# Top-32 attention and convolution stage: statistics, norms, reciprocals and the reversal put on other engines and into other steps

## The chip, the cores and the metric

One core of one Trainium2 chip runs the whole program. The metric is the device time of one execution in microseconds (us). The engines are TensorE (PE), VectorE (DVE), ScalarE (ACT), GpSimd (POOL) and SyncE (SP, which issues the DMAs here). They run their own instruction streams and meet in semaphores.

## The reference, cut to what matters

The program is four layers of gated cross-attention and feed-forward on x of 32 x 128 x 128 with a context of 32 x 128 x 96. The change touches the attention of layer 1 (32 batches of 128 tokens, 4 heads of 32):

```
scores = einsum('bthd,bghd->bhtg', Q, K) / sqrt(DH)
topv, topi = top_k(scores, 32);  probs = softmax(topv)
attn = zeros_like(scores).at[bi, hi, ti, topi].set(probs)
c_t = einsum('btg,bgd->btd', attn.mean(axis=1), V) * text_mask
x = layernorm(x_text, g_norm_in, b_norm_in)
scale_in, shift_in = split(c_t @ W_film_in + b_film_in, 2)
x = x * (1 + mod_gate * scale_in) + mod_gate * shift_in
y = s4d(x, ...)        # a causal convolution over the 128 tokens, one kernel per channel
```

Then a second FiLM with scale_out and shift_out, a residual and a feed-forward layer follow, and the later layers.

## The kernel before, in words

`build` runs six stages one after the other. `stage_film` is `film_in` (attention, first norm, FiLM; output x3, tokens in partitions, [128, channel, batch]) and then `convolve`. Between the two all engines meet in a barrier.

`film_in` works on pairs of batches (16 pairs) and on groups of 4 batches (8 groups, 512 columns). Every engine's order is written out by hand: a loop over p from -5 to 18 in which each engine does a fixed list of parts, for pair p+1, p, p-1 or p-2. The main parts:

- VectorE (lines 1455 to 1496): for pair p, four rounds of 8 MAX8 (`dve.max`, the 8 largest of 128 scores, one per head and batch) and 8 MATCH_REPLACE, which overwrites these 8 in `left`. After four rounds the 32 largest are gone from `left`. Ahead of an odd pair stand `group_stats` and `group_moments` (four BN_STATS and seven small operations by which the halves of BN_STATS are put together) for the norm of a later group, and three small operations for `rstd2`, the second variance (the norm is applied on a norm).
- ScalarE (1402 to 1453): for pair p-1 the exponential of `left` (`exb`), for pair p that of all scores (`exa`), each with the sum over the keys as a second output; for pair p+1 the evacuation of the scores (`sc`); for a group the evacuation of `xnT` (p odd) or of `kT` and `qT` (p even); for pair p-2 those of `wT`, `aT` and the FiLM product `fo`, two of each.
- GpSimd (1268 to 1337): the shift of the softmax (`shift`, from the first maximum); for a group the power for `rstd`, the application of the norm to four batches (`xn`, line 1297), two copies into `k.mean1` and `k.rstd1`, and the second norm with its gain and bias (x2); for pair p-1 the two differences (`share` = tota - totb, and exa - exb, which leaves the 32 largest), the power -1 (line 1322), two products; for pair p-2 the FiLM: x2 times f, plus f, written into `k.x3[:, :, i]`, 128 bytes between neighbours (1336).
- TensorE (1339 to 1400): for pair p-2 the head mean and its transposition (`wT`), for pair p+1 the scores, for a group the transpositions of `xn` and the K and Q products (banks 6 and 7), for pair p-2 `aT` and the FiLM product. All 8 banks of PSUM are in use; the scores have one buffer (banks 0 to 3).
- SP: the contexts, four of the eight chunks of Toeplitz matrices (1 MB each) at the start, and after each batch the half of `fo` that the next stage needs, to DRAM (`fo_dram`). It waits for the last of these at the end.

After the last pair VectorE quantizes a weight for a later stage (1498 to 1525), in exchange with TensorE.

`convolve` (1528 to 1584) first reverses x3 in the tokens, by a product with an exchange matrix `k.flip`: 8 chunks of 512 columns over TensorE, each evacuated by ScalarE into x3 in place. Then, chunk after chunk, 16 Toeplitz products with 32 columns of weights each, an evacuation, 4 transpositions, a copy by VectorE back into x3. Four chunks of Toeplitz matrices are loaded at its start (`v_late`).

Of the kernel before, what the change touches and what calls it, by code (L numbers as in the profile page):

```python
# [5 lines left out]
F32 = mybir.dt.float32  # L6
# [10 lines left out]
G = 4  # L17
# [1163 lines left out]
def stage_film(nc, w, ps, k):  # L1181

    with ExitStack() as ctx:
        k.toep = ctx.enter_context(nc.sbuf_tensor("v_toep", [128, EARLY, CH, 128], F32))
        once = ctx.enter_context(OneTime(nc, "v_in_"))
        k.toep_in = [once(f"toep_in{i}") for i in range(CHUNKS)]
        film_in(nc, w, ps, k)
        convolve(nc, w, ps, k)
# [5 lines left out]
def film_in(nc, w, ps, k):  # L1194
# [8 lines left out]
    TAKES = 2 * H * ROUNDS  # L1203
    with ExitStack() as ctx:
        def tmp(name, shape, dt=F32):
            return ctx.enter_context(nc.sbuf_tensor("c_" + name, shape, dt))

        nm = Norm(lambda n, s: ctx.enter_context(nc.sbuf_tensor(n, s, F32)), "c")
        rstd2 = tmp("rstd2", [128, 2, G])
# [4 lines left out]
        minus, tshare = tmp("minus", [128, H]), tmp("tshare", [128, B])  # L1214
        sc, left = tmp("sc", [128, 4, H, 128]), tmp("left", [128, 4, H, 128])
# [8 lines left out]
        stats, halves, square, mean, ve, rstd, rr, vr, ve2, rstd2_done, kept = (  # L1224
            once(n) for n in ("stats", "halves", "square", "mean", "ve", "rstd", "rr", "vr", "ve2", "rstd2_done",
                              "kept"))
# [9 lines left out]
        fo_out = [once(f"fo_out{i}") for i in range(2)]  # L1236
# [5 lines left out]
        norm = dict(stats=Signal(stats, 0, 2 * G, k.apart), halves=Signal(halves, 0, 6, k.apart),  # L1242
                    square=Signal(square, 0, 4, k.apart), mean=Signal(mean, 0, 2, k.apart),
                    ve=Signal(ve, 0, 2, k.apart))
# [7 lines left out]
        def _(sp):  # L1252
# [4 lines left out]
            for i in range(B):  # L1257
                if i in (10, 18):
                    e = i // 8 + 1
                    sp.wait_ge(aT_ps, 8 * (e - 1))  # L1260
                    sp.dma_start(cx[:, e % 2], c_dram[:, 8 * e:8 * e + 8, :]).then_inc(cx_in[e], 16)
                sp.wait_ge(fo_done, i + 1)
                sp.dma_start(k.fo_dram[:, i:i + 1, :].rearrange("s b c -> s (b c)"),
                             fo[:, i % 2, 256:512]).then_inc(fo_out[i % 2], 16)
            for a in range(2):
                sp.wait_ge(fo_out[a], 16 * B // 2)

        @block.gpsimd
        def _(pool):
# [3 lines left out]
            pool.memset(minus[:], -1.0).then_inc(consts, 1)  # L1273
            pool.tensor_scalar(tshare[:], k.tmask[:], 1.0 / H, None, ALU.mult).then_inc(consts, 1)
            pool.wait_ge(consts, 3)
# [4 lines left out]
            for p in range(FIRST, LAST):  # L1280
                for i in pair(p):

                    pool.wait_ge(top_done, TAKES * p + H * (i % 2 + 1))
                    if i >= 4:
                        pool.wait_ge(exb_done, H * (i - 3))
                    pool.tensor_scalar(shift[:, i % 4, :], first[:, i % 2, :, 0], -SCALE, None,
                                       ALU.mult).then_inc(shift_done, 1)
                if (p + 4) % 2 == 0 and 0 <= (p + 4) // 2 < GROUPS:
                    g = (p + 4) // 2
                    u = g % 2  # L1290
                    pool.wait_ge(ve, g + 1)
                    pool.tensor_tensor(nm.rstd[:, u], nm.ve[:, u], k.half[:, 0:G], ALU.pow).then_inc(rstd, 1)
                    pool.wait_ge(rstd, g + 1)
                    if g >= 4:
                        pool.wait_ge(x3_done, G * (g - 3))
# [3 lines left out]
                    pool.tensor_copy(k.mean1[:, G * g:G * g + G], nm.mean[:, u]).then_inc(kept, 1)  # L1299
                    pool.tensor_copy(k.rstd1[:, G * g:G * g + G], nm.rstd[:, u]).then_inc(kept, 1)  # L1300
# [14 lines left out]
                for i in pair(p - 1):  # L1315
                    a = i % 2
                    pool.wait_ge(exb_done, H * (i + 1))
                    pool.tensor_tensor(share[:, a, :], tota[:, i % 4, :], totb[:, a, :],
                                       ALU.subtract).then_inc(tot_done, 1)
# [1629 lines left out]
```

## Time and profile before

| | us |
|---|---|
| median of 3 runs | 1514.41 (1513.07 to 1514.45) |
| profiled execution | 1510.89 |
| its span, first to last instruction | 1509.1 |
| mean granted TensorE clock | 0.849 of full |
| opening of `film_in` | 207.1 to 223.4 |
| loop of 16 pairs on VectorE | 223.4 to 472.9 |
| rest of `film_in` to `convolve`'s first product | 472.9 to 494.3 |
| `convolve` to the first product of `stage_mix` | 494.3 to 518.7 |

Times are read from the span's start. A duration is that of the instruction; neighbours on an engine can overlap a little, so eight operations of 0.39 us may take 3.18 us together. The granted clock is 0.5 or 1.0 at any moment, which are TensorE's levels of 1.2 and 2.4 GHz; between them stand means over a stretch. The ends of matmuls are modelled.

### The profile page before, as it was taken

To read this page: it belongs to the slowest core of one execution; us is meant where nothing else is said; L and a number is where in the kernel's file an instruction comes from. 1 tells how busy PE (TensorE), PEld (TensorE's weight loads), DVE (VectorE), ACT (ScalarE), POOL (GpSimd) and SP (SyncE) were. 2 spreads that over 40 slices of the span, in tenths; PEclk is the share of its full clock that TensorE was granted. 3 is DMA by queue.
4 is the path that set the end of the run, shared out by engine and by line. 5 is a ranking of instruction groups with operands and counts; after the bars stand their busy time and mean duration, and the time that the engine had idled before them with its cause. 6 is when DMAs were issued, how large, how long until landed. Compare 5 with 4: busy or idle time off the path is not lost. (4 is left out here: it accounts for less than half of the span.)

```text
span 1509.1 us, 30794 instructions
## 1 busy us (share of the span) xinstructions
PE 1195.9 (79%) x10535; PEld 812.8 (54%) x10535; DVE 1009.3 (67%) x3919; ACT 684.5 (45%) x1990; POOL 594.7 (39%) x806
## 2 busy tenths in 40 slices
PE   4767654766676669885698988689999969999997
PEld 3433322443444445554476767356667657776765
DVE  6767759999996279862577777677776544444442
ACT  3343335566665344421244444356666633333332
POOL 4677576888867155530323231233433310000000
PEclk7789865566666779996699999799999979898988
DMA  6301050010000511100000000000000000000001
GB/s 164 90 1 43 1 134 1 15 32 16 25 22 22 161 43 27 30 16 16 1 3 3 3 3 3 1 1 1 2 2 2 1 1 0 1 0 0 0 0 56
DMA packets 63678, 35.54 MB, mean 24 GB/s; under 512 B 23925, under 2 KB 61424, under 8 KB 63538
## 3 DMA queue, kind: packets, MB, share of 16 engines
q1 hardware_dynamic: 62234, 33.45, 8.5%
q8 instruction: 76, 1.25, 0.4%
q14 instruction: 64, 0.52, 0.1%
q10 hardware_dynamic: 1304, 0.33, 0.1%
HBM read 25.21 MB, written 6.42 MB: 21 GB/s over the span
## 5 line engine op out<-in xcount | busy, mean ns | idle before, releaser
L2821 DVE SCALAR_TENSOR_TENSOR k_X<-ps,m_gt,k_X 128x128 f32 (+1 forms) x256 | 72.1, 345 | 123.0 <-PE ps L2720 123.0
L2750 ACT ACTIVATE m_hid<-ps,k_b 128x512 f32<-128x512 f32 x128 | 81.8, 684 | 134.9 <-PE ps L2720 127.7
L2720 PEld LDWEIGHTS ps<-k_w,m_hid 128*128 128x128 f32 x1024 | 123.1, 192 | 26.8 <-issue 17.2
L2711 PE MATMUL ps<-m_xnT,k_w 128*128 128x512 f32 x256 | 127.8, 630 | 1.1 <-DVE m_lg L2766 1.1
L2720 PE MATMUL ps<-k_w,m_hid 128*128 128x128 f32 x1024 | 123.4, 275 | 0.0
L2399 POOL TENSOR_TENSOR l_p<-l_p,l_rsum 128x512 f32<-128x512 f32 x64 | 65.2, 1039 | 139.4 <-DVE l_rsum L2658 139.4
L2259 DVE TENSOR_REDUCE g_top<-ps 128x8 f32<-128x1024 f32 x64 | 75.4, 1220 | 50.6 <-PE ps L2127 50.6
L1494 DVE MATCH_REPLACE8 c_left<-c_top,c_left 128x128 f32<-128x128 f32 x384 | 104.5, 354 | 0.0
L2519 ACT ACTIVATE l_p<-ps,l_shift 128x128 f32<-128x128 f32 x256 | 91.4, 389 | 21.3 <-DVE l_shift L2603 20.2
L2207 ACT ACTIVATE g_pT<-ps 128x1024 f32<-128x1024 f32 x64 | 62.0, 1021 | 84.8 <-PE ps L2143 84.8
L711 PE MATMUL ps<-f_expT,f_xeT 128*128 128x512 f32 x128 | 69.9, 675 | 29.3 <-DVE k_X L1089 29.0
L1488 DVE MAX8 c_top<-c_left 128x8 f32<-128x128 f32 x384 | 81.9, 349 | 0.0
L1367 PE MATMUL ps<-c_kT,c_qT 32*128 32x128 f32 x256 | 22.9, 440 | 72.9 <-ACT c_sc L1427 71.6
L121 POOL TENSOR_TENSOR m_rstd<-m_ve,k_half 128x8 f32<-128x8 f32 x4 | 6.6, 1639 | 186.0 <-DVE m_ve L114 186.0
L2711 PEld LDWEIGHTS ps<-m_xnT,k_w 128*128 128x128 f32 x256 | 47.5, 204 | 41.1 <-issue 39.6
L842 ACT ACTIVATE f_part<-ps,f_wf 128x128 f32<-128x128 f32 x128 | 36.3, 368 | 71.4 <-issue 46.1
L1353 PEld LDWEIGHTS ps<-k_ident,c_exa 128*128 128x128 f32 x256 | 48.9, 283 | 23.0 <-issue 12.4
L1494 DVE MATCH_VALUE_LOAD c_left<-c_top,c_left 128x8 f32 x384 | 60.1, 158 | 0.0
L711 PEld LDWEIGHTS ps<-f_expT,f_xeT 128*128 128x128 f32 x128 | 24.4, 214 | 66.0 <-DVE k_X L1089 46.3
L1367 PEld LDWEIGHTS ps<-c_kT,c_qT 32*128 32x128 f32 x256 | 14.9, 268 | 82.6 <-issue 77.1
L2519 ACT ACTIVATION_READ_ACCUMULATOR l_p<-ps,l_shift 128x1 f32 x256 | 58.8, 230 | 0.0
L1089 DVE SCALAR_TENSOR_TENSOR k_X<-ps,f_wf,k_X 128x128 f32<-128x128 f32 x128 | 44.6, 349 | 19.8 <-PE ps L711 15.8
(535 smaller groups left out, 3284.3 us busy)
## 6 DMA issues: line engine op xcount, KB each, us to landing
v_toep<-kpad SPq DMA_DIRECT2D x4, 1024.0 KB, 10.5
fo_dram<-c_fo SPq DMA_DIRECT2D x32, 128.0 KB, 1.7
v_late<-kpad SPq DMA_DIRECT2D x4, 1024.0 KB, 10.1
d_fo<-fo_dram SPq DMA_DIRECT2D x8, 512.0 KB, 3.6
k_X<-in_x SPq DMA_DIRECT2D x8, 256.0 KB, 3.4
out<-k_X SPq DMA_DIRECT2D x4, 512.0 KB, 5.4
f_cx<-in_ctx SPq DMA_DIRECT2D x4, 384.0 KB, 5.6
c_cx<-in_ctx SPq DMA_DIRECT2D x4, 384.0 KB, 4.7
```

Source lines behind the costliest of these rows:

```text
L711: pe.matmul(ps[:, 4 + (2 * b + h) % 3, :], xeT[:, t % 2, u, cols], expT[:, 4 * h:4 * h + 4, :].rearrange("p e d -> p (e d)"), start=True, ...
L1353: m = pe.matmul(ps[:, 4 + a, 0:128], exa[:, i % 4, h, :], k.ident[:], start=h == 0, stop=h == H - 1)
L1488: dve.max((first if r == 0 else top)[:, a, h, :], (sc if r == 0 else left)[:, i % 4, h, :]).then_inc(top_done, 1)
L1494: dve.match_replace(left[:, i % 4, h, :], (first if r == 0 else top)[:, a, h, :], (sc if r == 0 else left)[:, i % 4, h, :], TAKEN).then_in ...
L2207: act.activation(pT[:, n % 2, 2 * h:2 * h + 2, :].rearrange("p a n -> p (a n)"), ps[:, 4 + 2 * h:6 + 2 * h, :].rearrange("p a n -> p (a n) ...
L2259: dve.tensor_reduce(top[:, (n + 1) % 2, :].rearrange("p (r c) -> p r c", r=R)[:, 2 * h:2 * h + 2, 0:R], ps[:, 2 * h:2 * h + 2, :].rearrang ...
L2399: pool.tensor_tensor(p[:, n % 3, 4 * a:4 * a + 4, :], p[:, n % 3, 4 * a:4 * a + 4, :], rsum[:, n % 3, 4 * a:4 * a + 4].rearrange("p (h o) ...
L2519: act.activation(p[:, i % 3, h, :], ps[:, 2 * (i % 2) + a, 128 * b:128 * b + 128], ACT.Exp, bias=shift[:, i % 2, h:h + 1], scale=SCALE, ac ...
L2711: pe.matmul(ps[:, 4 * u + q, :], k.w1_3[:, e, 128 * q:128 * q + 128], xnT[:, u], start=True, stop=True).then_inc(s["hid_ps"].sem, 1)
L2720: m = pe.matmul(ps[:, 4 * u + 2 + e % 2, j * S:j * S + S], hid[:, u, q, j * S:j * S + S], k.w2_3[:, e, q, :], start=q == 0, stop=q == 1)
L2750: act.activation(hid[:, u, q, :], ps[:, 4 * u + q, :], ACT.Gelu, bias=k.b1_3[:, 2 * e + q:2 * e + q + 1]).then_inc(s["hid"].sem, 1)
L2821: dve.scalar_tensor_tensor(out=xj[u][j], in0=ps[:, 4 * u + 2 + e % 2, j * S:j * S + S], scalar=gt[:, u, j, e:e + 1], in1=xj[u][j], op0=ALU ...
```

## The change

- **Statistics.** VectorE's `group_moments` is replaced by one BN_AGGREGATE per batch (`dve.bn_aggr`), which gives mean and variance into `k.mv1`; the addition of eps, the power and the `rstd2` arithmetic are GpSimd's.
- **Norms.** The application of the norm moves from GpSimd to VectorE for groups 0 and 1, and to ScalarE for the others (an ACTIVATE with scale rstd and bias -mean x rstd, at the end of its even steps).
- **Reciprocals.** GpSimd's two powers -1 per pair become one RECIPROCAL of 128x8 on VectorE, for pair p-1, ahead of round 2 of pair p, behind a wait for GpSimd's differences. GpSimd makes these differences right behind the shift.
- **Opening.** The statistics of groups 0 and 1 and their applications come first on VectorE, those of group 2 stand in round 1 of pair 0; the K product and evacuation of group 0 come before its transpositions.
- **Reversal.** GpSimd writes the FiLM result contiguously into `y` (two batches). Three steps after the pair, at the end of TensorE's step, one product of 256 columns reverses it in bank 7, and ScalarE copies it into x3 with `p (a c) -> p c a`. The eight products and evacuations of `convolve` go.
- **Loads.** `sc` and `left` lie in memory that outlives `film_in`; the Toeplitz chunks 4 and 5 are loaded into them before the end of the stage, so `v_late` holds two chunks. The wait for the `fo_dram` DMAs moves into `convolve`.

```diff
+        st, nshift, rstd2 = tmp("st", [128, 2, G, 6]), tmp("nshift", [128, B]), tmp("rstd2", [128, 2, G])
+        sc, left = (t[:].rearrange("p (i h) s -> p i h s", h=H) for t in (k.sc, k.left))
+        y = tmp("y", [128, 2, 128])
@@ sync, in the loop over the batches
+                if i == B - 4:
+                    sp.wait_ge(left_done, TAKES * (PAIRS - 1) + 2 * H)
+                    sp.wait_ge(exa_done, H * B)
+                    load_toeplitz(sp, k, EARLY, k.sc[:])
                 sp.wait_ge(fo_done, i + 1)
...
+                if i == B - 2:
+                    sp.wait_ge(exb_done, H * B)
+                    load_toeplitz(sp, k, EARLY + 1, k.left[:])
-            for a in range(2):
-                sp.wait_ge(fo_out[a], 16 * B // 2)
@@ gpsimd
+                for i in pair(p - 1):
+                    a = i % 2
+                    pool.wait_ge(exb_done, H * (i + 1))
+                    if i >= 2:
+                        pool.wait_ge(part_done, i - 1)
+                    pool.tensor_tensor(share[:, a, :], tota[:, i % 4, :], totb[:, a, :],
+                                       ALU.subtract).then_inc(tot_done, 1)
+                    pool.tensor_tensor(exa[:, i % 4], exa[:, i % 4], exb[:, a], ALU.subtract).then_inc(diff_done, 1)
                 if (p + 4) % 2 == 0 and 0 <= (p + 4) // 2 < GROUPS:
...
+                    pool.wait_ge(mv_done, G * (g + 1))
+                    pool.tensor_scalar(k.rstd1[:, of], k.mv1[:, of, 1], EPS, None, ALU.add).then_inc(ve, 1)
                     pool.wait_ge(ve, g + 1)
+                    pool.tensor_tensor(k.rstd1[:, of], k.rstd1[:, of], k.half[:, 0:G], ALU.pow).then_inc(rstd, 1)
                     pool.wait_ge(rstd, g + 1)
-                    for j in range(G):
-                        pool.tensor_scalar(xn[:, g % 4, j, :], k.X[:, G * g + j, :], nm.mean[:, u, j:j + 1],
-                                           nm.rstd[:, u, j:j + 1], ALU.subtract, ALU.mult).then_inc(xn_done, 1)
+                    if g >= EARLY_GROUPS:
+                        pool.tensor_tensor(nshift[:, of], k.mv1[:, of, 0], k.rstd1[:, of], ALU.mult).then_inc(nmr, 1)
+                        pool.wait_ge(nmr, g - EARLY_GROUPS + 1)
+                        pool.tensor_scalar(nshift[:, of], nshift[:, of], -1.0, None, ALU.mult).then_inc(nshift_done, 1)
...
-                    pool.tensor_tensor(share[:, a, :], share[:, a, :], minus[:], ALU.pow).then_inc(inv_done, 1)
+                    if a == 0:
+                        pool.wait_ge(inv_done, p)
...
-                    pool.tensor_tensor(k.x3[:, :, i:i + 1], x2.rearrange("p (c o) -> p c o", o=1),
-                                       f[:, 128:256].rearrange("p (c o) -> p c o", o=1), ALU.add).then_inc(x3_done, 1)
+                    if i >= 2:
+                        pool.wait_ge(flip_ps, i // 2)
+                    pool.tensor_tensor(y[:, i % 2, :], x2, f[:, 128:256], ALU.add).then_inc(x3_done, 1)
@@ tensor, last in each step (FLIP = 3)
+                if pair(p - FLIP):
+                    i = 2 * (p - FLIP)
+                    pe.wait_ge(x3_done, i + 2)
+                    pe.wait_ge(kT_done, min((p + 2) // 2 + 1, GROUPS))
+                    if i:
+                        pe.wait_ge(flipped, i // 2)
+                    pe.matmul(ps[:, 7, 0:256], k.flip[:], y[:].rearrange("p a c -> p (a c)"), start=True,
+                              stop=True).then_inc(flip_ps, 1)
@@ scalar, last in each step
+                if pair(p - FLIP):
+                    i = 2 * (p - FLIP)
+                    act.wait_ge(flip_ps, i // 2 + 1)
+                    act.activation(k.x3[:, :, i:i + 2], ps[:, 7, 0:256].rearrange("p (a c) -> p c a", a=2),
+                                   ACT.Identity).then_inc(flipped, 1)
+                if (p + 4) % 2 == 0 and EARLY_GROUPS <= (p + 4) // 2 < GROUPS:
+                    g = (p + 4) // 2
+                    act.wait_ge(nshift_done, g - EARLY_GROUPS + 1)
+                    if g >= 4:
+                        act.wait_ge(x3_done, G * (g - 3))
+                    for j in range(G):
+                        i = G * g + j
+                        act.activation(xn[:, g % 4, j, :], k.X[:, i, :], ACT.Identity, bias=nshift[:, i:i + 1],
+                                       scale=k.rstd1[:, i:i + 1]).then_inc(xn_done, 1)
@@ vector
+            def moments(g):
...
+                for j in range(G):
+                    dve.bn_stats(st[:, g % 2, j, :], k.X[:, G * g + j, :]).then_inc(stats, 1)
+                for j in range(G):
+                    dve.wait_ge(stats, G * g + j + 1)
+                    dve.bn_aggr(k.mv1[:, G * g + j, :], st[:, g % 2, j, :]).then_inc(mv_done, 1)
...
+            def inverses(p):
+                dve.wait_ge(tot_done, 2 * p + 2)
+                dve.reciprocal(share[:].rearrange("p a h -> p (a h)"),
+                               share[:].rearrange("p a h -> p (a h)")).then_inc(inv_done, 1)
+            for g in range(EARLY_GROUPS):
+                moments(g)
+            for g in range(EARLY_GROUPS):
+                apply(g)
+            for p in range(PAIRS):
+                if p % 2 == 1 and (p + 5) // 2 < GROUPS:
+                    moments((p + 5) // 2)
+                for r in range(ROUNDS):
+                    if p == 0 and r == 1:
+                        moments(2)
+                    if p >= 1 and r == 2:
+                        inverses(p - 1)
@@ convolve
-            for c in range(CHUNKS):
-                pe.matmul(ps[:, c, :], k.flip[:], chunk(c), start=True, stop=True).then_inc(flip_ps, 1)
...
-            for c in range(CHUNKS):
-                act.wait_ge(flip_ps, c + 1)
-                act.activation(chunk(c), ps[:, c, :], ACT.Identity).then_inc(flipped, 1)
```

## Rows read from the trace of the kernel before

**Rows 1.** Windows view, the loop; columns as its header says, then TensorE's clock, DMA, GB/s

```profile
core 0: us, PE busy (x) PEld busy (x) DVE busy (x) ACT busy (x) POOL busy (x), PEclk, DMA share, GB/s
...
223.37:472.85 249.48, 155.98 (x733) 94.64 (x734) 248.46 (x1611) 151.91 (x628) 195.53 (x304) 0.62 0.07 21
```

**Rows 2.** Timeline of VectorE in the loop: start us, us, engine, line, operation

```profile
237.85 0.91 DVE L97 BATCH_NORM_STATS2 c_stats<-k_X 128x6 f32<-128x128 f32 x4
...
240.08 1.07 DVE L1488 MAX8 c_first<-c_sc 128x8 f32<-128x128 f32 x5
...
254.56 0.73 DVE L1488 MAX8 c_first<-c_sc 128x8 f32<-128x128 f32 x3
...
302.33 1.24 DVE L180 TENSOR_TENSOR c_mean<-c_stats 128x4 f32<-128x4 f32 x1
```

**Rows 3.** Waits of ScalarE, 271 to 477 us: total us, times, longest us

```profile
ACT c_fo L1453 <- PE ps L1395: 34.9, 27, 1.7
...
ACT c_exa L1420 <- POOL c_shift L1286: 4.3, 3, 1.9
```

**Rows 4.** Timeline of ScalarE: first `c_exb` of seven steps

```profile
271.47 0.39 ACT L1413 ACTIVATE c_exb<-c_left,c_shift 128x128 f32<-128x128 f32 x1
...
287.54 0.39 ACT L1413 ACTIVATE c_exb<-c_left,c_shift 128x128 f32<-128x128 f32 x1
...
305.31 0.39 ACT L1413 ACTIVATE c_exb<-c_left,c_shift 128x128 f32<-128x128 f32 x1
...
320.41 0.39 ACT L1413 ACTIVATE c_exb<-c_left,c_shift 128x128 f32<-128x128 f32 x1
...
385.82 0.39 ACT L1413 ACTIVATE c_exb<-c_left,c_shift 128x128 f32<-128x128 f32 x1
...
401.31 0.39 ACT L1413 ACTIVATE c_exb<-c_left,c_shift 128x128 f32<-128x128 f32 x1
...
476.15 0.39 ACT L1413 ACTIVATE c_exb<-c_left,c_shift 128x128 f32<-128x128 f32 x1
```

**Rows 5.** Windows view, three short stretches

```profile
298.00:305.00 7.00, 6.15 (x12) 2.70 (x11) 6.83 (x40) 2.29 (x8) 6.69 (x11) 0.50 0.05 18
...
396.00:401.30 5.30, 4.30 (x15) 1.77 (x14) 5.23 (x30) 2.82 (x8) 5.14 (x8) 0.93 0.00 0
...
492.00:494.00 2.00, 0.00 (x0) 0.00 (x0) 0.00 (x0) 0.00 (x0) 0.44 (x1) 0.59 0.19 66
```

**Rows 6.** Timeline of VectorE and ScalarE in the stage after (stage_mix)

```profile
526.04 0.36 DVE L1916 BATCH_NORM_AGGREGATE d_mv<-d_st 128x2 f32<-128x6 f32 x4
...
521.41 3.18 ACT L1852 ACTIVATE d_u<-k_X,d_nmr,k_rstd 128x128 f32<-128x128 f32 x8
...
520.88 0.38 ACT L1838 ACTIVATE d_mwd2T<-ps 128x256 f32<-128x256 f32 x1 [4.76 <-PE ps L1729]
```

**Rows 7.** Timeline of GpSimd and ScalarE in the opening

```profile
210.28 3.15 POOL L1297 TENSOR_SCALAR c_xn<-k_X,c_mean,c_rstd 128x128 f32<-128x128 f32 x4
...
219.72 0.60 ACT L1427 ACTIVATE c_sc<-ps 128x512 f32<-128x512 f32 x1 [1.01 <-PE ps L1370]
```

**Rows 8.** Timeline of GpSimd and TensorE at the stage's end

```profile
491.98 0.46 POOL L1336 TENSOR_TENSOR k_x<-c_xn,c_fo 128x128 f32<-128x128 f32 x1
...
494.32 9.51 PE L1550 MATMUL ps<-k_x,k_flip 128*128 128x512 f32 x16 [3.67 <-PEq L72]
...
503.76 1.50 PE L1558 MATMUL ps<-v_toep,k_x 128*32 128x128 f32 x46
```

**Rows 9.** Lines view, GpSimd in the loop and VectorE in stage_mix: count, busy us, mean ns

```profile
L1336 POOL TENSOR_TENSOR k_x<-c_xn,c_fo 128x128 f32<-128x128 f32 x32 | 14.7, 461 | 2.5
...
L1334 POOL TENSOR_TENSOR c_xn<-c_xn,c_fo 128x128 f32<-128x128 f32 x32 | 14.6, 456 | 34.4 <-ACT c_fo L1453 34.4
...
L1936 DVE TENSOR_TENSOR d_z<-k_x,d_fo 128x512 f32<-128x512 f32 x7 | 7.1, 1009 | 0.0
...
L1939 DVE TENSOR_TENSOR d_z<-d_z,d_u 128x512 f32<-128x512 f32 x8 | 5.5, 693 | 1.4 <-POOL d_u L1699 1.2
```

More of the change, by code:

```diff
@@ L1186, in stage_film @@
         k.toep_in = [once(f"toep_in{i}") for i in range(CHUNKS)]
+        k.fo_out = [once(f"fo_out{i}") for i in range(2)]
+        k.sc = ctx.enter_context(nc.sbuf_tensor("v_sc", [128, CH, 128], F32))
+        k.left = ctx.enter_context(nc.sbuf_tensor("v_left", [128, CH, 128], F32))
         film_in(nc, w, ps, k)
@@ L1223, in film_in @@
         consts, zero_aT, cx_in = once("consts"), once("zero_aT"), [once(f"cx_in{i}") for i in range(4)]
-        stats, halves, square, mean, ve, rstd, rr, vr, ve2, rstd2_done, kept = (
-            once(n) for n in ("stats", "halves", "square", "mean", "ve", "rstd", "rr", "vr", "ve2", "rstd2_done",
-                              "kept"))
+        stats, mv_done, ve, rstd, nmr, nshift_done, rr, vr, ve2, rstd2_done = (
+            once(n) for n in ("stats", "mv_done", "ve", "rstd", "nmr", "nshift_done", "rr", "vr", "ve2",
+                              "rstd2_done"))
         xn_done, x2a, x2b, x2c, xT_ps, xT_done, q_ps, k_ps, qT_done, kT_done = (
@@ L1241, in film_in @@
                               "wmag_done", "wr_done", "wr_T", "identb_done"))
-        norm = dict(stats=Signal(stats, 0, 2 * G, k.apart), halves=Signal(halves, 0, 6, k.apart),
-                    square=Signal(square, 0, 4, k.apart), mean=Signal(mean, 0, 2, k.apart),
-                    ve=Signal(ve, 0, 2, k.apart))
+        flip_ps, flipped = once("flip_ps"), once("flipped")
         block = ctx.enter_context(nc.Block())
@@ L1373, in _ @@
                     g = (p + 3) // 2
+                    if g == 0:
+                        pe.matmul(ps[:, 7, :], k.wk1[:], k.cT[:, 0:W], start=True, stop=True).then_inc(k_ps, 1)
                     pe.wait_ge(xn_done, G * (g + 1))
@@ L1383, in _ @@
                         pe.wait_ge(kT_done, g)
[L1384 removed]
+                        if p > FLIP:
+                            pe.wait_ge(flipped, p - FLIP)
+                        pe.matmul(ps[:, 7, :], k.wk1[:], k.cT[:, W * g:W * g + W], start=True, stop=True).then_inc(k_ps, 1)
                     pe.wait_ge(xT_done, g + 1)
@@ new lines, in moments, with apply @@
+            def moments(g):
+                if g >= 2:
+                    dve.wait_ge(mv_done, G * (g - 1))
+                for j in range(G):
[3 more added lines that the diff above has]
+                    dve.bn_aggr(k.mv1[:, G * g + j, :], st[:, g % 2, j, :]).then_inc(mv_done, 1)
+            def apply(g):
+                dve.wait_ge(rstd, g + 1)
+                for j in range(G):
+                    i = G * g + j
+                    dve.tensor_scalar(xn[:, g % 4, j, :], k.X[:, i, :], k.mv1[:, i, 0:1], k.rstd1[:, i:i + 1],
+                                      ALU.subtract, ALU.mult).then_inc(xn_done, 1)
@@ L1543, in _ @@
         def _(sp):
-            for c in range(EARLY, CHUNKS):
-                load_toeplitz(sp, k, c, late[:, c - EARLY])
+            for c in range(EARLY + 2, CHUNKS):
+                load_toeplitz(sp, k, c, late[:, c - EARLY - 2])
+            for a in range(2):
+                sp.wait_ge(k.fo_out[a], 16 * B // 2)
         @block.tensor
         def _(pe):
-            for c in range(CHUNKS):
-                pe.matmul(ps[:, c, :], k.flip[:], chunk(c), start=True, stop=True).then_inc(flip_ps, 1)
             for n in range(CHUNKS + 1):
                 if n < CHUNKS:
-                    pe.wait_ge(flipped, n + 1)
                     pe.wait_ge(k.toep_in[n], 16)
-                    toep = k.toep[:, n] if n < EARLY else late[:, n - EARLY]
+                    toep = (k.toep[:, n] if n < EARLY else k.sc[:] if n == EARLY else k.left[:] if n == EARLY + 1
+                            else late[:, n - EARLY - 2])
                     for i in range(CH):
```

73 lines of the change are left out of this document (25 added, 48 removed).

## The prediction

> **What bounds the kernel now.** I read the loop's stretch first, then VectorE's timeline inside it, then ScalarE's waits and the starts of its steps, and last the opening and the end of the stage. In the loop of the top-32 attention VectorE is busy 248.46 of 249.48 us, while TensorE is granted a mean clock of 0.62 [rows 1]. That looks like a loop bound by VectorE. A pair of batches costs VectorE 14.48 us, from the first MAX8 at 240.08 to that at 254.56 [rows 2], so 16 pairs cost 232 us; the other 17.4 us are the statistics and the variance arithmetic of later groups, five blocks of them and a short one. Part of these is waiting: a 128x4 addition lasted 1.24 us [rows 2].
>
> ScalarE is just as full in another sense: its order is fixed and most of it hangs on TensorE. From 271 to 477 us it waits 34.9 us for the FiLM product and 4.3 for GpSimd's shift [rows 3], some more for other products of TensorE, and never for VectorE. I call a step the time between the first `c_exb` of one pair and that of the next. A step with the query transposition takes 320.41 - 305.31 = 15.10 us, one with kT and qT 305.31 - 287.54 = 17.77 us, or 401.31 - 385.82 = 15.49 us [rows 4] where TensorE was granted the high level in its second half (0.93, against 0.50 in the slow one [rows 5]). Two such steps make 32.9 us, against 2 x 14.5 + 3.3 = 32.3 us for VectorE. So the two are level, and it is ScalarE's last step, from 476.15, that the rest of the stage hangs on.
>
> **The change, part by part.** A(k) is the start of `c_exb` for pair k.
>
> *Opening, to A(2).* Four BN_AGGREGATE lasted 0.36 us together [rows 6] behind four BN_STATS of 0.91 [rows 2], overlapping a little: 1.15 us per group. GpSimd's application began at 210.28 [rows 7] behind a block about 0.5 us longer, so the first factors stand near 209.8; four applications on VectorE, which I put at 0.8 to 1.5 us, end near 211.0 instead of 213.4, where GpSimd's four took 3.15 us [rows 7]. The Q product no longer stands behind the K product (0.5 us more). So the first scores are evacuated by 217.4, where it was 220.3 [rows 7], and the second, 1.7 us later, by 219.1. VectorE began at 223.37 [rows 1], because moments(2) stood in front; it now begins at 217.4 and loses 0.9 us waiting for the second batch: 5.1 us earlier. moments(2) inside round 1 takes 1.15 of that, so A(0) is 3.9 us earlier. moments(3) costs 1.15 where the block from 237.85 to 240.08 cost 2.2 [rows 2], and a reciprocal 0.2 by my estimate, two of those BN_AGGREGATEs of 0.09, so A(1) is 4.7 us earlier. The next step is ScalarE's own, 17.77 plus four applications of 1.55 us: A(2) moves from 271.47 [rows 4] to 268.2, **-3.3 us**.
>
> *Loop, A(2) to A(15), 13 steps.* On VectorE 17.4 us become 5 x 1.15 + 15 x 0.2 = 8.8 us, 8.6 less, and GpSimd loses a power per batch and an application per group. I count both at nothing, since ScalarE's longer order covers them; if it did not, they would be the gain (first rival). ScalarE gets two things. The application of a group, four ACTIVATEs: eight of that form took 3.18 us [rows 6], so 1.55 to 1.6 us, in four of these steps: 6.2 us. And the flip copy at the end of every step: eight 512-column products made 9.51 us at mixed clock [rows 8], at the low level 1.7 us each, so 0.86 us for 256 columns; it is queued behind the second FiLM product, ScalarE is through with `c_fo` 0.5 us after that product, waits 0.4 us and copies. A 128x256 evacuation lasted 0.38 us [rows 6], 0.35 in a row of them: 0.75 us x 13 = 9.75 us. Bounds: 0.33 us (product hidden under `c_fo`) and 1.2 us (a copy of twice the length). I take 0.75 because the clock is low at that place in most steps. In return the 4.3 us of waiting for the shift [rows 3] go, since VectorE is early. Together **+11.6 us**.
>
> The new wait on VectorE (`tot_done`, before round 2) has two rounds of 14.48 / 4 = 3.62 us queued behind it. GpSimd has both sums 3.6 us after a step begins, so VectorE ends its pair 11 us after it. The next step needs that only after 15 us; the scores of the next pair stand at 8.6. VectorE will idle there, 2 to 4 us a pair, at no cost unless steps get shorter than 11 us. GpSimd, 195.53 us busy in the loop [rows 1], gets lighter and stays covered. SP's two moved loads stand behind waits for pair 15; the FiLM output DMAs behind them are late by nothing that is waited for before the convolution.
>
> *End of the stage.* From A(15) to the last x3 took 492.44 - 476.15 = 16.3 us [rows 4, 8]. The reciprocals shorten GpSimd's part by 2 us, but the last aT product stands behind the transposition of the quantized weights on TensorE's queue, so I count that at nothing. The last additions wait for the flip of the pair before (+0.3), the last flip and copy add 1.3 us, and less contention for VectorE's quantization gives back 0.8: **+0.8 us**. The wait for the FiLM output DMAs leaves the end of the block: **-0.4 us**.
>
> *Convolution.* It began at 494.32, and its first Toeplitz product at 503.76 [rows 8], behind eight flips. Those 9.4 us go entirely if TensorE is at 2.4 GHz when it begins. The granted clock in the 2 us after the last work was 0.59 [rows 5], so it fell about 2.5 us after the last product; the new gap is some 2.4 us. If it has fallen, some 4.7 us run at half speed and 2.2 us are given back. Two chunks are left to load, against four, and all land before their turn. I take **-9.4 us**.
>
> **Sum:** -3.3 + 11.6 + 0.8 - 0.4 - 9.4 = -0.7 us against the profiled execution's 1510.89 us: 1510.2. The median of the runs shown, 1514.41, is 3.5 us above it, so I forecast 1513.7 us, no change. About 0.2% (3 us) is what a measurement of this kernel can tell from none.
>
> **Rivals.**
> (1) *VectorE stays the bound.* Then 8.6 us in the loop, 3.9 in the opening and 9.8 at the end come off, with little on ScalarE: about 21 us less, 1493. For it: 248.46 of 249.48 us busy [rows 1]. Against it: ScalarE's steps follow each other with no wait for VectorE [rows 3], and each gets longer. Chance 0.06.
> (2) *Faster by clock and hiding.* Of six steps with kT and qT, two had the high level in their second half and were 2.2 us shorter [rows 4, 5]. If four of the five left are so (two more, -4.4 us), or the flip ends under `c_fo` (13 x 0.4 = -5.2 us), the time is 1508.5 to 1509.3. For it: TensorE's unbroken run of products around `c_fo` gets 0.9 us longer. Chance 0.30.
> (3) *Slower: the flip copy is dear.* It reads PSUM with 512 bytes between neighbours and writes x3 in pieces of 8 bytes, 128 bytes apart. GpSimd's strided write of x3 cost nothing (461 against 456 ns), but VectorE's strided read of x3 made a 128x512 operation 1009 instead of 693 ns [rows 9]. If the copy takes 0.75 instead of 0.35 us, 13 x 0.4 = 5.2 us come on top: 1518.9. It decides from 0.29 us more per step on. A clock that stays low in all five kT-qT steps (+4.4, 1518.1) lands in the same place and is in this chance: 0.28. The Trainium skill (SBUF — State Buffer, "Specifications (TRN2)") gives 16-byte lines in SBUF and 8-byte lines in PSUM, with a penalty for each crossing to a new line; by that rule this rival is the outcome. The trace agrees for VectorE's read, not for GpSimd's write, and no row shows ScalarE's.
> (4) *The forecast.* Chance 0.36.
>
> **How the numbers follow.** Faster is rivals 1 and 2, 0.36; same 0.36; slower 0.28. The range takes in the clock (-6.6 to +4.4), the flip (-5.5 to +5.9) and the convolution's clock (0 to +2.2), which do not all fall one way: about -8.5 to +8 around the sum, 1505 to 1521.5. The first rival stays outside.
>
> **What would show it.** ScalarE's steps: 15.9 us where they were 15.1, 19.3 to 20.1 where they were 17.8, and no idle time before `c_exb`. VectorE idle before the reciprocal, 2 us or more per pair, and busy under 92% of the loop. The flip copy at 0.38 us behind a wait of 0.4. The first scores at 217, the convolution beginning near 502 and lasting 15 us. I am wrong if ScalarE waits for VectorE before `c_exb`, or VectorE shows no idle time: then the loop shrinks. A copy of 0.7 us or more speaks for the third rival.

## Result and the profile after

The changed kernel takes 1508.39 us, the median of 20 runs (1504.14 to 1514.05). The kernel before took 1512.51 us in 20 runs beside them (1509.43 to 1516.99). The ratio is 0.9973, with a 95% interval of 0.9963 to 0.9984: 0.27% or 4.1 us faster, just over the 0.2% (3 us) that the prediction had named as the limit of no change. The forecast was 1513.7 us and no change; the measured time lies inside its range, 5.3 us below the forecast.

The profiled execution took 1509.82 us, only 1.1 us less than that of before. First, the windows view of it; columns as its header says.

```profile
core 0: us, PE busy (x) PEld busy (x) DVE busy (x) ACT busy (x) POOL busy (x), PEclk, DMA share, GB/s
219.44:475.00 255.56, 153.46 (x782) 93.80 (x783) 236.17 (x1569) 165.49 (x664) 154.37 (x275) 0.67 0.09 26
...
0.00:205.00 205.00, 138.28 (x762) 77.57 (x762) 142.93 (x517) 80.03 (x225) 125.31 (x209) 0.79 0.23 55
```

VectorE is busy 236.17 of 255.56 us, 92.4%, where it was busy 99.6% [rows 1]. It works less, and the loop is no shorter. The second line is the code ahead of the stage, which the change does not touch: there TensorE got a mean clock of 0.79, where the same window of before had 0.83, and the stage starts 2.3 us later. So I compare the two traces from the first BN_STATS of `film_in` on (207.16 before, 209.43 after). From there `stage_mix` begins after 311.55 us before and 304.63 after: the stage itself got 6.9 us shorter.

The waits, first ScalarE's, then VectorE's: total us, times, longest us.

```profile
ACT c_fo L1488 <- PE ps L1417: 35.1, 28, 1.7
ACT v_sc L1458 <- PE ps L1388: 15.0, 14, 1.1
...
ACT c_exb L1444 <- DVE v_left L1558: 8.4, 2, 6.0
...
ACT k_x L1492 <- PE ps L1430: 2.2, 9, 0.3
```

```profile
DVE c_share L1525 <- POOL c_share L1301: 18.6, 9, 4.2
DVE c_first L1552 <- ACT v_sc L1458: 4.7, 2, 3.9
```

ScalarE waits for TensorE's FiLM product about as long as before (33.8 us from A(2) to A(15), for 34.9 [rows 3]; the line above covers a longer stretch), the wait for GpSimd's shift is gone, and VectorE holds up its `c_exb` only in the first two steps. VectorE now idles 18.6 us in nine waits ahead of its new reciprocal. That is the picture the prediction drew. TensorE waits too, for ScalarE to empty the one buffer of the scores (223 to 477 us):

```profile
PE ps L1385 <- ACT v_sc L1458: 82.8, 15, 9.9
```

The starts of ScalarE's steps show where time came from. Step k is the time from A(k) to A(k+1). First `c_exb` of pairs 2, 3, 4 and 15, and three ends of steps, from ScalarE's timeline (start us, us):

```profile
267.89 0.39 ACT L1444 ACTIVATE c_exb<-v_left,c_shift 128x128 f32<-128x128 f32 x1
...
282.50 0.60 ACT L1488 ACTIVATE c_fo<-ps 128x512 f32<-128x512 f32 x1 [1.11 <-PE ps L1417]
283.29 0.40 ACT L1492 ACTIVATE k_x<-ps 128x256 f32<-128x256 f32 x1 [0.19 <-PE ps L1430]
283.58 0.39 ACT L1444 ACTIVATE c_exb<-v_left,c_shift 128x128 f32<-128x128 f32 x1
...
301.70 0.40 ACT L1492 ACTIVATE k_x<-ps 128x256 f32<-128x256 f32 x1 [0.26 <-PE ps L1430]
301.99 1.63 ACT L1501 ACTIVATE c_xn<-k_X,c_nshift,k_rstd 128x128 f32<-128x128 f32 x4
303.52 0.39 ACT L1444 ACTIVATE c_exb<-v_left,c_shift 128x128 f32<-128x128 f32 x1
...
334.48 0.60 ACT L1488 ACTIVATE c_fo<-ps 128x512 f32<-128x512 f32 x1 [0.26 <-PE ps L1417]
334.97 0.40 ACT L1492 ACTIVATE k_x<-ps 128x256 f32<-128x256 f32 x1
...
480.70 0.39 ACT L1444 ACTIVATE c_exb<-v_left,c_shift 128x128 f32<-128x128 f32 x1
```

A step without kT is 283.58 - 267.89 = 15.69 us (15.10 before [rows 4]); one with kT, qT and the application 303.52 - 283.58 = 19.94 us. In step 5, at 334.48, the FiLM wait is 0.26 instead of 1.11 us, the flip is not waited for, and the step is 17.50 us. The granted clock of the slow and of the fast step, and then of the second half of each, by the windows view:

```profile
283.58:303.52 19.94, 14.17 (x62) 8.41 (x61) 19.94 (x136) 12.41 (x48) 15.63 (x30) 0.66 0.06 21
319.27:336.77 17.50, 12.43 (x73) 7.85 (x76) 16.45 (x111) 12.25 (x48) 15.68 (x30) 0.77 0.08 25
...
293.00:303.52 10.52, 9.66 (x23) 5.41 (x22) 10.52 (x72) 5.09 (x13) 7.08 (x13) 0.50 0.07 25
...
328.00:336.77 8.77, 7.77 (x34) 4.32 (x36) 8.77 (x61) 4.92 (x13) 7.83 (x13) 0.84 0.10 32
```

Last, the stage's end: ScalarE's last copy and the convolution's first products, from the timeline, and two windows of the convolution.

```profile
496.15 0.38 ACT L1492 ACTIVATE k_x<-ps 128x256 f32<-128x256 f32 x1 [1.85 <-PE ps L1430]
...
497.64 3.26 PE L1624 MATMUL ps<-v_toep,k_x 128*32 128x128 f32 x64 [1.53 <-PEq L72]
```

```profile
497.64:514.01 16.37, 14.40 (x288) 11.34 (x288) 5.53 (x8) 4.78 (x8) 0.00 (x0) 0.90 0.60 162
497.70:502.00 4.30, 4.30 (x80) 3.74 (x84) 0.16 (x1) 1.19 (x2) 0.00 (x0) 0.60 1.01 269
```

The Toeplitz products come first in the convolution, but in their first 4.3 us the granted clock is 0.60. The convolution takes 16.4 us where it took 24.4.

The stage in four pieces (us), worked out from the starts of `c_exb`, of the convolution and of `stage_mix`. From here on A(2) and A(15) are counted from the stage's first BN_STATS, so A(15) is 268.99 before and 271.27 after:

```
                             before   after   change   forecast
to A(2)                       64.31   58.46    -5.85      -3.3
A(2) to A(15), 13 steps      204.68  212.81    +8.13     +11.6
A(15) to the convolution      18.17   16.94    -1.23      +0.4
convolution                   24.39   16.42    -7.97      -9.4
sum                          311.55  304.63    -6.92      -0.7
```

The 6.9 us are not all seen in the time: from the start of `stage_mix` on, with the same code but for the place from which the norm's mean is read, the profiled execution of before needs 990.4 us and that of the changed kernel 993.9. These 3.5 us are lost in `stage_mix` alone, and the forecast had nothing for them. Part is a wait for the first load of the FiLM output; first `d_z` on VectorE, before and after:

```profile
522.30 1.03 DVE L1936 TENSOR_TENSOR d_z<-k_x,d_fo 128x512 f32<-128x512 f32 x1 [3.07 <-DMA d_fo<-fo_dram]
```

```profile
519.00 1.02 DVE L1999 TENSOR_TENSOR d_z<-k_x,d_fo 128x512 f32<-128x512 f32 x1 [4.43 <-DMA d_fo<-fo_dram]
```

That wait is 3.96 to 4.97 us in all ten traces of this study with the reversal in the steps, and 2.95 to 3.20 in the four with it in the convolution. The rest of the program takes 993.0 to 994.3 us in nine of those ten (991.3 in act_again) and 990.3 to 990.6 in three of those four (996.3 in u_flip). So some 3 us of what the reversal saves seem to go again in the stage behind it; why the load lands later, and what makes the rest, was not tried.

### The profile page after: what moved, and what is told of

Its sections match the earlier page's. It is cut to its first block and busy times, and to the rows that moved or that the text cites. A ratio compares the mean times of both kernels' runs of the same rounds, so it can differ in the third digit from the quotient of the medians.

```text
span 1508.0 us, 30865 instructions
## 1 busy us (share of the span) xinstructions
PE 1190.6 (79%) x10551; PEld 809.9 (54%) x10551; DVE 994.8 (66%) x3895; ACT 693.8 (46%) x2022; POOL 546.9 (36%) x769
## 5 line engine op out<-in xcount | busy, mean ns | idle before, releaser
L2582 ACT ACTIVATE l_p<-ps,l_shift 128x128 f32<-128x128 f32 x256 | 91.4, 390 | 20.9 <-DVE l_shift L2666 18.6
L1558 DVE MATCH_REPLACE8 v_left<-c_top,v_left 128x128 f32<-128x128 f32 x384 | 100.9, 276 | 0.0
L711 PE MATMUL ps<-f_expT,f_xeT 128*128 128x512 f32 x128 | 77.2, 739 | 27.2 <-DVE k_X L1089 27.1
L1552 DVE MAX8 c_top<-v_left 128x8 f32<-128x128 f32 x384 | 77.9, 275 | 0.0
L2190 PE MATMUL ps<-g_kT,g_mq 32*128 32x128 f32 x1024 | 39.4, 291 | 18.5 <-POOL g_mq L2168 10.9
L1444 ACT ACTIVATE c_exb<-v_left,c_shift 128x128 f32<-128x128 f32 x128 | 49.3, 390 | 8.4 <-DVE v_left L1558 8.4
```

What stands on the lines that cost most here:

```text
L711: pe.matmul(ps[:, 4 + (2 * b + h) % 3, :], xeT[:, t % 2, u, cols], expT[:, 4 * h:4 * h + 4, :].rearrange("p e d -> p (e d)"), start=True, ...
L1444: act.activation(exb[:, i % 2, h, :], left[:, i % 4, h, :], ACT.Exp, bias=shift[:, i % 4, h:h + 1], scale=SCALE, accum_out=totb[:, i % 2, ...
L1552: dve.max((first if r == 0 else top)[:, a, h, :], (sc if r == 0 else left)[:, i % 4, h, :]).then_inc(top_done, 1)
L1558: dve.match_replace(left[:, i % 4, h, :], (first if r == 0 else top)[:, a, h, :], (sc if r == 0 else left)[:, i % 4, h, :], TAKEN).then_in ...
L2582: act.activation(p[:, i % 3, h, :], ps[:, 2 * (i % 2) + a, 128 * b:128 * b + 128], ACT.Exp, bias=shift[:, i % 2, h:h + 1], scale=SCALE, ac ...
```

## Experiments

**What is to be told apart.** The theory: ScalarE's fixed order, tied to TensorE, sets the loop, and VectorE's relief of 8.6 us is hidden by it. Its rival is the prediction's first: VectorE is the bound. The first three kernels undo one part each, the fourth tests the prediction's third rival, and the later ones turn ScalarE's order round. No kernel puts VectorE's old statistics back by themselves.

### Powers back on GpSimd

```diff
-                dve.wait_ge(tot_done, 2 * p + 2)
-                dve.reciprocal(share..., share...)
+                    pool.tensor_tensor(share[:, a, :], share[:, a, :], minus[:], ALU.pow)
```

> The changed kernel with the two powers -1 per pair back on GpSimd (1.02 us each) and no reciprocal on VectorE. If ScalarE's chain sets the loop: A(2) to A(15) stays at 212 to 214 us, VectorE's 23 us of waiting for the sums go from ahead of the reciprocal to ahead of the scores of the next pair, and the time stays within 3 us of the changed kernel, 1508. If VectorE's waiting is what the loop costs: the 23 us come off, 1485 to 1490.

Measured: 1508.4 us (10 runs), ratio to the kernel before 0.9975 (0.9963 to 0.9986). The steps from A(2) on are those of the changed kernel within 0.45 us each, and A(15) comes at 271.06 us for 271.27. VectorE's idle time has only moved, from the reciprocal to the scores (its waits, 223 to 470 us):

```profile
DVE c_first L1552 <- ACT v_sc L1460: 15.2, 12, 4.4
```

So the reciprocal's place is worth nothing here, and VectorE waits for ScalarE at either place.

### Application back on GpSimd

```diff
-                        act.activation(xn[:, g % 4, j, :], k.X[:, i, :], ACT.Identity, bias=nshift[:, i:i + 1], scale=...)
+                            pool.tensor_scalar(xn[:, g % 4, j, :], k.X[:, i, :], k.mv1[:, i, 0:1], ..., ALU.subtract, ALU.mult)
```

> The changed kernel with the application of groups 2 to 7 back on GpSimd (3.15 us per group there). If ScalarE's chain sets the loop: each kT-qT step loses 1.6 us, five of them behind A(1), so 8 us less, 1500.5. If VectorE or GpSimd sets it: no change or slower, 1508 to 1515.

Measured: 1507.39 us, ratio 0.9976 (0.9964 to 0.9988), no different from the changed kernel. Steps 3, 5, 7 and 9 are all 18.41 us, 1.5 less than the changed kernel's 19.94, as the theory has it. But the changed kernel has two fast steps of 17.5 us, 5 and 9, and here the second half of both is at a granted clock of 0.50; and step 2, with a wait for GpSimd's shift in it, grows to 17.74. So A(15) comes only 2.0 us sooner, not 8, and the end of the stage takes 2.2 us more: the 1.55 us per application is right for a step at one level and does not carry to the sum.

### Reversal back in the convolution

```diff
-                    pe.matmul(ps[:, 7, 0:256], k.flip[:], y[:].rearrange("p a c -> p (a c)"), ...)
-                    act.activation(k.x3[:, :, i:i + 2], ps[:, 7, 0:256].rearrange("p (a c) -> p c a", a=2), ACT.Identity)
+            for c in range(CHUNKS):
+                pe.matmul(ps[:, c, :], k.flip[:], chunk(c), start=True, stop=True)
```

> The changed kernel with the reversal back in the convolution (eight products and evacuations there, none in the steps). If ScalarE's chain sets the loop: the 13 steps give back 0.3 to 0.65 us each, about 7, the end of the stage 1.3, and the convolution costs 8 more: within 2 us of the changed kernel, 1508. If the steps' flips are hidden: the 8 us stay, 1516.

Measured: 1512.9 us, ratio 1.0014 (0.9996 to 1.0031), 4.5 us above the changed kernel by the medians and between the two times that I had named. This one part carries the whole gain: without it the change is worth nothing that can be measured. The steps of both kernels, from the starts of `c_exb`:

```
step        2      3      4      5      6      7      8      9     10     11     12     13     14
changed 15.69  19.94  15.75  17.50  15.39  19.95  15.75  17.44  15.75  18.42  14.35  14.36  12.52
u_flip  15.10  19.31  15.12  19.31  15.11  19.31  15.11  19.31  15.11  17.78  14.07  14.07  11.88
```

A flip costs 0.28 us in steps 12 and 13 and 0.64 us in most others. But in u_flip steps 5 and 9 take 19.31 us like steps 3 and 7, with a granted clock of 0.50 in their second halves, and the 13 steps sum to 210.59 us against 212.81: the kernel with the flips loses 2.2 us in the loop. It saves 8 us in the convolution.

### Is the strided copy dear?

```diff
-                    act.activation(k.x3[:, :, i:i + 2], ps[:, 7, 0:256].rearrange("p (a c) -> p c a", a=2), ...)
+                    act.activation(k.x3[:, 4 * i:4 * i + 8, :].rearrange("p c b -> p (c b)"), ps[:, 7, 0:256], ...)
```

> The changed kernel with the reversal's copy reading and writing without gaps; what it leaves wrong in place is the order of x3's elements, so the convolution and all behind it work on other numbers, with the same instructions. If ScalarE's strided access cost anything (the third rival), the copy falls below the 396 ns that it takes in the changed kernel, and the loop shortens by 13 times the difference. If, as I now think, it costs nothing, the copy stays between 380 and 396 ns, the steps at 15.7, 17.4 or 19.9 and 14.35 us, and the time within 2 us of the changed kernel.

Measured: 1506.47 us (7 runs), ratio 0.9959 (0.994 to 0.9979), steps as in the changed kernel, A(15) at 271.11. The copy by the lines view, in the changed kernel and then here: count, busy us, mean ns.

```profile
L1492 ACT ACTIVATE k_x<-ps 128x256 f32<-128x256 f32 x16 | 6.3, 394 | 4.1 <-PE ps L1430 4.1
```

```profile
L1492 ACT ACTIVATE k_x<-ps 128x256 f32<-128x256 f32 x16 | 6.1, 383 | 4.2 <-PE ps L1430 4.2
```

A read of PSUM with 512 bytes between neighbours and a write in pieces of 8 bytes, 128 apart, cost ScalarE 11 ns of 394. The prediction's third rival, a copy of 0.75 us, is refuted by the copy's own time.

### ScalarE's order, first try

If ScalarE's order is the bound and VectorE has room, another order should let the loop fall to VectorE's own 14.6 us a pair. The first try takes each half's scores as soon as they can be there:

```diff
-  exb, exa, sc (0 and 1), xnT, kT, qT, wT, aT, fo, flip, xn
+  sc0, exb0, sc1, exb1, xnT, kT, wT, exa0, qT, aT, exa1, fo0, xn, fo1, flip
```

> The changed kernel with ScalarE's step in another order: the four groups of exponentials (1.55 us each) are put between operations that wait for TensorE (after the first scores, after the second, after wT, after aT), and the application between the two FiLM evacuations. Same work on every engine. If ScalarE's chain of waits for TensorE sets the loop: its steps fall below VectorE's 14.7 to 15.9 us per pair, VectorE becomes the bound with no idle time, and A(15) comes about 18 us earlier: 1488 to 1492. If the loop is set by ScalarE's or VectorE's amount of work, or the new order makes new waits: 1505 to 1512.

Measured: 1504.67 us, ratio 0.9966 (0.9954 to 0.9979), 13 us above the expectation. Steps 2, 4, 6 and 8 are 14.6 to 14.9 us, steps 3, 5, 7 and 9, those with kT and qT, 19.24. Its longest waits, of ScalarE, of TensorE and of GpSimd:

```profile
ACT v_sc L1443 <- PE ps L1388: 60.0, 11, 8.3
```

```profile
PE ps L1371 <- POOL c_exa L1345: 34.1, 7, 11.5
```

```profile
POOL c_share L1301 <- ACT c_exb L1450: 33.1, 12, 3.3
```

ScalarE waits up to 8.3 us for scores that TensorE has queued behind the transpositions of the weights; these wait for GpSimd's products, which need the exponentials `exb`, and these stand behind the scores on ScalarE. The in-order queues (each engine takes its operations in the order in which they are written) had closed into a ring, with GpSimd in it.

### Exponentials first, with both orders and alone

`exb` goes back ahead of the scores here, half by half, to open that ring; the other places change a little as well. GpSimd's order is changed as well in one kernel (products with the share ahead of the norm and x2) and left in the other. The third puts both orders on the kernel before, the fourth has the powers on GpSimd. Odd and even in the orders and expectations below go by the loop's p, which is one more than the number of the step: its even steps are steps 3, 5, 7 and 9 here.

```diff
-  exb, exa, sc (0 and 1), xnT, kT, qT, wT, aT, fo, flip, xn
+  exb0, sc0, exb1, sc1, wT, exa0, xnT, kT, (odd steps: aT), exa1, qT, (even steps: aT), xn, fo, flip
```

> The changed kernel with two orders turned round: ScalarE takes each half's exponential of the second operand as soon as it can and its scores behind it, the products of the weights before the transposes; and GpSimd makes the products with the share (which TensorE's queue waits for) ahead of the norm's product and the application. Theory A (the loop is set by in-order queues that wait for one another, not by an engine's work): with no queue held up, VectorE's own work of 13.9 us a pair becomes the bound, each step is 14 to 15 us, scores wait on ScalarE no longer, and the stage ends about 15 to 20 us sooner: 1487 to 1493 us. Theory B (the granted clock falls or TensorE's own work is the bound, so that another order only moves the waits): steps of 15.7 and 19 us stay on average, 1503 to 1507 us.

> ScalarE's order of order2 alone, GpSimd's order as in the changed kernel. Theory A: the wait for the scores stays, since TensorE's queue has the weights' products ahead of them and these wait for GpSimd's part: even steps of 17 to 19 us, odd ones near 15; 1498 to 1505 us. Theory B: as order2.

> The kernel before with both new orders, so with VectorE's old work of 16.5 us a pair. Theory A: VectorE, busy over 98% in the loop, is the bound; its pairs take 16 to 17 us as they did, and the kernel gains little: 1500 to 1511 us, some 14 to 20 us above order2. It would show that the change's savings on VectorE pay only once ScalarE's order lets them. Theory B: the same time as order2 within 8 us.

> order2 with the reciprocal of the totals back on GpSimd. Theory A: GpSimd's part of a pair comes some 1 to 2 us later to TensorE while VectorE has 0.8 us less a pair: within 5 us of order2, slower if GpSimd's part is what TensorE waits for, faster by up to 10 us (0.8 x 13) if VectorE alone is the bound. Theory B: no difference to order2 over 2 us.

```
               median us  ratio to before (95%)       steps in the loop   A(15)
order2           1492.12  0.9842 (0.9808 to 0.9875)   14.3 and 15.9       249.76
order2_act       1488.94  0.9849 (0.9818 to 0.9881)   14.6 and 15.6       249.77
order2_recip     1488.49  0.9829 (0.9807 to 0.9851)   14.9 and 15.2       248.76
order2_before    1517.03  1.0023 (1.0008 to 1.0039)   14.5 and 19.4       270.02
```

A(15) comes 21.5 us sooner than in the changed kernel as soon as ScalarE's order lets it, with the same work on every engine. Windows view of order2_act, and in a second fence the longest of ScalarE's waits:

```profile
223.37:460.00 236.63, 148.78 (x768) 94.68 (x767) 234.14 (x1559) 161.78 (x673) 156.17 (x277) 0.71 0.08 25
```

```profile
ACT c_exb L1444 <- DVE v_left L1584: 37.7, 16, 7.9
```

VectorE is busy 99% again, and ScalarE waits for it in 16 places: here VectorE is the bound. The granted clock (0.71) did not stand in the way, so theory B falls. TensorE's wait for the scores' buffer, 82.8 us in the changed kernel, is now

```profile
PE ps L1385 <- ACT v_sc L1451: 26.4, 14, 7.9
```

In the changed kernel the scores' evacuations stand behind all 16 exponentials, and TensorE stands still for them; here those of the first batch stand behind four and those of the second behind eight, and the other exponentials fill the time in which ScalarE waited for TensorE. GpSimd's order is not needed, and my expectation for order2_act was 9 us too high: the ring of the first try is open without it. Which of ScalarE's places matters most was not taken apart. order2_recip, within 4 us of order2 as expected and with intervals that overlap, shows the reciprocal's place to be worth nothing under this order either.

On the kernel before the same orders gain nothing (1517.0 us, where I had expected up to 1511). VectorE is its bound there (ScalarE waits 61.4 us for it), with 14.5 us a pair and 4.8 us for each block of statistics; in order2_act VectorE's pairs, from first MAX8 to first MAX8, take 15.65 us with a block and 14.58 without, 1.07 for the block. So with the new orders the change brings A(15) 20 us sooner (270.02 to 249.76), some 5 of them by A(1), and ScalarE's old order hides most of this: with the old order the change is worth 4.1 us, with both new ones 1517.0 - 1492.1 = 25 us. Two things make that number uncertain. The old block costs only 3.1 to 3.7 us in the kernel before, so the new orders made it dearer, and the old kernel was not tried with ScalarE's new order alone.

### Which parts pay under the new order

act_flip and act_xn make on order2_act the edits shown for u_flip and u_xn; act_again is order2_act, timed a second time.

> order2_act with the reversal of x3 back in the convolution (eight 512-column products and copies ahead of it) and without the flips in the steps. With VectorE as the loop's bound the in-step flips are hidden, so the steps stay at 14.6 and 15.6 us and A(15) at 249.8 us, and the whole 8.0 us by which the convolution got shorter come back: 1495 to 1499 us. If the flips in the steps still cost what they did in the changed kernel (0.3 to 0.65 us each), the loop gives 4 to 5 us back and it lands at 1491 to 1494.

> order2_act with the application of the norm back on GpSimd. With VectorE as the bound neither engine's share of the work is seen: steps of 14.6 and 15.6 us, A(15) at 249.8 us, and within 2 us of order2_act (1487 to 1491). If GpSimd's part of a pair comes late by its 3.2 us, ScalarE waits for its shift in the even steps and A(15) comes up to 3 us later.

> order2_act once more, for its time: 1487 to 1491 us, 1.3 to 1.7% less than the kernel before and 1.1 to 1.4% less than the changed one. If the first measurement, of four runs, was a lucky one, it comes to 1492 or more.

act_again took 1488.5 us (4 runs), ratio 0.9855 (0.9836 to 0.9875): the gain of 1.45% over the kernel before stands; against the changed kernel it is 1 - 0.9855/0.9973 = 1.2%.

act_flip took 1495.41 us, ratio 0.9902 (0.9879 to 0.9925). A(15) stays at 249.75 us, so the flips in the steps cost nothing now, and the time is 6.9 us longer than that of act_again. That is 0.5% by the ratios, where the same edit cost 0.4% under the old order.

act_xn took 1499.53 us, ratio 0.992 (0.9904 to 0.9937), which I had not expected: 11 us slower, with A(15) at 258.35. The longest wait of ScalarE and of TensorE in it:

```profile
ACT v_sc L1454 <- PE ps L1391: 38.1, 12, 7.3
```

```profile
PE ps L1374 <- POOL c_exa L1348: 30.3, 6, 6.6
```

GpSimd's four applications, 3.15 us in every other step, stand ahead of its products, TensorE's queue stands behind these, and the scores come late for VectorE, whose pairs grow to as much as 17.45 us. What was worth nothing in the changed kernel is the dearer of the two parts taken away here. The norm on ScalarE pays by the time that it gives GpSimd.

## Why the prediction was right and where it missed

**The bound.** Right. VectorE's idle time ahead of the reciprocal, its share of 92%, ScalarE's steps and the lack of a wait for VectorE are as described; u_recip agrees that VectorE's relief is hidden, and order2_act shows it, since another order of ScalarE's same work sets it free. The first rival (1493 us) is refuted for this kernel. It describes the kernel with the new order.

**Opening (-3.3 forecast, -5.85 measured).** A(1) came 5.3 us sooner for 4.7: VectorE's first MAX8 is 6.2 us sooner by the stage's clock, for 6.0. The step from A(1) to A(2) was to be 17.77 + 1.55 = 19.3 us and is 17.25, because TensorE had the high level in part of it, and ScalarE's waits for its aT and FiLM products were 2 us shorter. What failed is "the next step is ScalarE's own, 17.77 plus four applications": the 17.77 was a step at the low level, and that level did not stay. The windows view of that step, before and after:

```profile
253.69:271.47 17.78, 10.04 (x28) 4.76 (x29) 17.71 (x113) 10.50 (x42) 14.86 (x21) 0.50 0.02 8
```

```profile
250.64:267.89 17.25, 9.36 (x44) 4.95 (x48) 17.25 (x116) 12.00 (x47) 13.78 (x25) 0.70 0.04 15
```

**Loop (+11.6 forecast, +8.1 measured).** The application cost its 1.55 us where the level was the same. The flip, taken at 0.75 us, cost 0.28 to 0.64 by u_flip: the copy adds 0.29 us, the time from its start to that of what follows, and not the 0.35 of its length; and the wait for the product, with ScalarE's lost overlap, adds 0.3 to 0.35 and in some steps nothing, not 0.4 in all. That is the term that was mis-sized. The shift waits stood in steps 2, 6 and 10 of before (16.07, 16.84 and 17.06 us, against 15.1 in u_flip): 4.7 us came off, where 4.3 were forecast. The four applications are 1.5 us each, 6.1 (6.2). What is left of the 8.1 us, 6.7, is the 13 flips, for the 9.75 of the forecast. The clock did little to the sum here: steps 5 and 9 are the fast ones in both kernels (15.70 and 15.49 us before, 17.50 and 17.44 after). That it could have done much is seen in u_xn and u_flip, which lost both.

**End of the stage (+0.4 forecast, -1.2 measured).** The last copy is through at 496.53, and the convolution starts at 497.64. u_flip, which has no flip in this piece, takes 16.3 us from A(15) to the convolution, where before took 18.2 and the changed kernel 16.9. So the last flips cost 0.6 us, for the 1.6 forecast, and the other parts of the change save 1.9, for 1.2; 0.6 of these are the reciprocal's place, which was counted at nothing (u_recip takes 17.6 us); no run takes the other 1.3 apart.

**Convolution (-9.4 forecast, -8.0 measured).** The bound named for a fallen clock, 2.2 us given back, came true for the most part: 1.4 us, with a granted clock of 0.60 in the first 4.3. The reading behind it was off: in before TensorE's last product ended at 490.65 (3.67 us of idle time ahead of 494.32 [rows 8]), and with 0.59 over the window from 492 [rows 5] the clock fell about 1.7 us after it, not 2.5. The gap, put at 2.4 us, is 1.53.

**The sum.** Three of the four terms were taken too dear, by 7.6 us together, and the convolution too cheap by 1.4: 6.2 us, so that the stage gained 6.9 us for the 0.7 forecast. The 3.5 us that `stage_mix` lost are in no term. The second rival, faster by clock and hiding, 1508.5 to 1509.3 us with a chance of 0.30, comes nearest to the 1508.39 measured, by both of its means: some 2 us by the high level in the step to A(2) and 3 us by a flip that is partly hidden. That the numbers agree so closely is in part luck: the forecast stood on a median of 1514.41 for the kernel before, and 20 runs put it at 1512.51, so 1.9 of the 5.3 us between forecast and measurement are not the change's. That the time fell inside the range is owed to the range's 16 us and to errors that partly cancelled.

**Third rival.** Refuted by c_dense: 394 against 383 ns. The Trainium skill (SBUF — State Buffer, "Specifications (TRN2)") states a penalty for each crossing to a new line, without a size. The measurement decides: on ScalarE's copy of 256 elements from PSUM to SBUF the strides cost 11 ns in all, 3%.

## What to carry to other kernels

An engine that is busy 99% need not be the only bound, and an engine's relief may be hidden by another engine's order. To see what a change can be worth, follow which wait ends last in each step, and look for in-order queues that wait for one another. In the changed kernel ScalarE and TensorE do so in turn; in the first try of a new order ScalarE's evacuations stood ahead of what GpSimd needed, to feed TensorE, to make what ScalarE was waiting for. Another order of ScalarE's same operations turned a gain of 0.27% into 1.45%, and a part that had shown nothing, the norm's place, was then worth 11 us: such parts should be judged together with the order that hides them, not alone.

## What was unexpected of the hardware

**TensorE's level may go with the work around it.** Of steps with the same operations some ran in 17.5 and some in 19.9 us, with a granted clock of 0.84 and 0.50 in their second halves. The changed kernel, u_recip and c_dense all have the fast steps 5 and 9; u_flip, without the flip product of 256 columns, and u_xn, without ScalarE's applications, have neither. But the kernel before, which has neither of the two operations, has the same fast steps. That is one trace of each kernel, and what decides the level was not isolated. A term of a sum that takes a step's time from a row holds only at that row's level.

**Small VectorE operations were longer beside a rearranged GpSimd.** The lines view of order2_before has one 128x4 operation at a mean of 766 ns, where the kernel before had it at 540 in the same stretch (200 to 500 us), and a block of statistics costs 4.8 us for 3.1 to 3.7. That GpSimd's work next to it is the cause was not tried.

```profile
L182 DVE TENSOR_TENSOR c_d<-c_diff 128x4 f32<-128x4 f32 x8 | 6.1, 766 | 0.3
```

**A record's length is not its pitch.** The pitch is the time from one start to the next. In the kernel before, a MAX8 of the later rounds has a mean of 349 ns from 200 to 500 us, and in order2_before 277 ns, with one pair in 14.48 and 14.53 us. The pitch is what counts for VectorE's path.

```profile
L1488 DVE MAX8 c_top<-c_left 128x8 f32<-128x128 f32 x384 | 81.9, 349 | 0.0
```

```profile
L1514 DVE MAX8 c_top<-c_left 128x8 f32<-128x128 f32 x384 | 78.6, 277 | 0.0
```
